# A gated linear-attention block with a ternary FFN on one core: probabilities, attention rows and first-norm rows split as rows and turned by transposing transfers

## The reference

```python
def step(carry, inp):
    mem, z = carry
    q_s, k_s, v_s = inp
    sq = jax.nn.elu(q_s) + 1.0
    att_mem = sq @ mem / (sq @ z)
    sk = jax.nn.elu(k_s) + 1.0
    mem = mem + jnp.einsum('bhlk,bhlv->bhkv', sk, v_s)
    z = z + sk.sum(axis=-2, keepdims=True).transpose(0, 1, 3, 2)
    att_dot = jax.nn.softmax(jnp.einsum('bhik,bhjk->bhij', q_s, k_s) * scale, axis=-1)
    att = att_dot @ v_s
    att = gate * att_mem + (1.0 - gate) * att
    return ((mem, z), att)
...
x = _layernorm(x + _L0_attn_ref(x, ...))     # its output: outs @ Wo
h = jax.nn.relu(jnp.einsum('bsd,fd->bsf', x, Wq1) + b1)
x = _layernorm(x + jnp.einsum('bsf,df->bsd', h, Wq2) + b2)
```

## Time and profile before

| | |
|---|---|
| median of 3 runs | 1882.06 us (1880.45 to 1883.52) |
| the profiled execution | 1882.23 us, its span 1880.3 us |
| TensorE busy | 1836.9 us, 98% |
| VectorE, ScalarE, GpSimd busy | 1448.7, 1004.3, 772.1 us (77%, 53%, 41%) |
| transfers | 117.47 MB in 556420 packets, 32.7% of 16 engines' time |
| mean granted clock of TensorE | 0.994 of full |

### The profile page before, as it was taken

One profiled execution on the slowest core, in us unless ns is written; L12 is line 12 of the kernel. 1 busy time (PEld: TensorE's weight loads), 2 busy tenths in 40 slices (PEclk: granted clock), 3 DMA queues, 4 the chain that ended last, 5 costly groups with the idle time before them and its releaser, 6 DMA issues.

```text
span 1880.3 us, 44342 instructions
## 1 busy us (share of the span) xinstructions
PE 1836.9 (98%) x16447; PEld 1305.1 (69%) x16447; DVE 1448.7 (77%) x2927; ACT 1004.3 (53%) x2422; POOL 772.1 (41%) x775
## 2 busy tenths in 40 slices
PE   5789999999999999999999999999999999999998
PEld 3666677776677776677776677776677776677765
DVE  7767877778877777877778877778877778877774
ACT  5765555555555555555555555555555555555541
POOL 1214334444334444334444334444334444334442
PEclk9899999999999999999999999999999999999999
DMA  8422433423433333333323343323333323333110
GB/s 274 125 39 37 65 59 62 67 42 56 67 59 60 67 47 51 66 57 62 68 42 56 66 60 60 67 41 57 65 62 60 67 39 59 61 63 63 34 24 23
DMA packets 556420, 117.47 MB, mean 62 GB/s; under 512 B 529824, under 2 KB 533808, under 8 KB 555696
## 3 DMA queue, kind: packets, MB, share of 16 engines
q1 hardware_dynamic: 556208, 114.64, 32.7%
HBM read 50.54 MB, written 16.80 MB: 36 GB/s over the span
## 4 chain that ended last, share of the span: by engine, by line
PE 95%; DVE 3%; ACT 1%; DMA 1%; POOL 0%; issue 0%; POOLq 0%; SPq 0%; DVEq 0%; ACTq 0%
PE bank L462 12%; PE bank L463 12%; PE bank L446 12%; PE bank L447 12%; PE bank L282 6%; PE bank L283 6%; PE bank L284 6%; PE bank L296 3%; PE bank L425 3%; PE bank L426 3%; PE bank L427 3%; PE bank L377 3%; PE bank L349 3%; PE bank L298 3%; PE bank L297 3%; PE bank L412 2%
## 5 line engine op out<-in xcount | busy, mean ns | idle before, releaser
L446 PE MATMUL bank<-yt,w1t 128*128 128x256 f16 x2048 | 453.9, 273 | 0.2 <-DVE yt L828 0.2
L447 PE MATMUL bank<-yt,w1t 128*128 128x256 f16 x2048 | 453.9, 273 | 0.0
L1157 ACT ACTIVATE prob<-bank,exp_bias,gscalars 128x128 f32<-128x128 f32 x512 | 227.7, 455 | 348.6 <-DVE exp_bias L745 346.8
L462 PE MATMUL bank<-w2t,arena 128*128 128x512 f16 x1024 | 388.4, 379 | 0.0
L463 PE MATMUL bank<-w2t,arena 128*128 128x512 f16 x1024 | 388.1, 379 | 0.0
L1201 ACT ACTIVATE arena<-bank,b_scaled,wscalars 128x256 f32<-128x256 f32 x512 | 262.9, 570 | 194.9 <-PE bank L447 123.8
L1326 POOL TENSOR_TENSOR att_mem<-att_mem,gate_in 128x512 f32<-128x512 f32 x60 | 76.2, 1271 | 356.7 <-DVE att_mem L784 356.7
L446 PEld LDWEIGHTS bank<-yt,w1t 128*128 128x128 f16 x2048 | 200.4, 98 | 23.4 <-ACT w2t L1226 0.3
L447 PEld LDWEIGHTS bank<-yt,w1t 128*128 128x128 f16 x2048 | 200.4, 98 | 22.8
L880 DVE CAST arena<-arena 128x512 f16<-128x512 f32 x256 | 159.6, 624 | 53.1 <-ACT arena L1201 52.4
L1404 POOL TENSOR_TENSOR arena<-arena 128x512 f16<-128x512 f32 x128 | 155.3, 1213 | 73.9 <-DVE arena L880 73.9
(11 more groups left out here) (184 smaller groups left out, 4324.5 us busy)
## 6 DMA issues: line engine op xcount, KB each, us to landing
rows<-in_L_attn_x SPq DMA_DIRECT2D x32, 512.0 KB, 3.9
out_rows<-rows SPq DMA_DIRECT2D x64, 256.0 KB, 2.3
x_blocks<-in_L_attn_x SPq DMA_DIRECT2D x248, 64.0 KB, 3.1
sk<-sk_t SPq DMA_DIRECT2D x480, 32.0 KB, 2.0
att_dot<-att_mem SPq DMA_DIRECT2D x480, 32.0 KB, 2.0
y_blocks<-rows SPq DMA_DIRECT2D x480, 32.0 KB
arena<-in_L_ffn_W SPq DMA_DIRECT2D x6, 1024.0 KB, 5.9
w2t<-in_L_ffn_W SPq DMA_DIRECT2D x2, 1024.0 KB, 13.1
```

The lines of the kernel that those rows point to most:

```text
L446: pe.matmul(ps[:, c], w1t[:, k, cols], yt[:, g % 2, :, k], start=k == 0, stop=False)
L447: ins = pe.matmul(ps[:, c], w1t[:, k, cols], yt[:, g % 2, :, KT + k], start=False, stop=k == KT - 1)
L462: pe.matmul(banks[own][:], h_hi[:, f, toks], w2t[:, f, :], start=f == 0, stop=False)
L1157: ins = act.activation(prob[:, t, at], ps[:, c], ACT.Exp, scale=gcol(g, G_EXP), bias=exp_bias[:, t, at:at + 1], accum_out=row_sum[:, t, h: ...
```

## The change

Three things are turned by a transposing transfer (`dma_start_transpose`) from SP, and their split into hi and lo is made before the turn, in rows:

- Probabilities: the exponentials write into the bank of the scores itself. `p_hi` (ScalarE) copies the bank to p_rows in float16, `p_lo` (VectorE) writes the rest beside it, and one transfer per sequence turns 128x2048 values into pt. TensorE's `turn_p` is gone, and a bank of scores is free only after p_lo.
- Attention rows and first-norm rows of groups 1 to 30: `at_hi`, `at_lo`, `yt_hi`, `yt_lo` work on rows, and one transfer per sequence turns 128x1024 values. The block moves and VectorE's turns of both are gone. The edge groups stay on TensorE.
- Order: both `scores` stand together on TensorE, then four pieces of `ffn_down`, then the V projections; VectorE has both score_max of a sequence together, group_max behind the first norm, and the p_lo between them; ScalarE has yt_hi in the middle of the exponentials and at_hi earlier; GpSimd has yt_lo before gate_mix.

```diff
@@ TensorE
             def scores(g, t):
-                    bank_free[b] = (sem["pexp"], by_half(g, t, e))
+                    bank_free[b] = (sem["pt_lo"], by_half(g, t, e))
-            def turn_p(g, t, half):
-                b = take(("p", g, t, half))
-                ps = banks[b][:].rearrange("p (h t) -> p h t", h=4)
-                pe.wait_ge(sem["pexp"], by_half(g, t, half))
-                for i in range(4):
-                    ins = pe.transpose(ps[:, i], prob[:, t, 4 * half + i], ident32[:])
-                ins.then_inc(sem["pturn"], 1)
-                bank_free[b] = (sem["pt"], by_half(g, t, half))
             def attend(g, t):
-                pe.wait_ge(sem["pt"], by_half(g, t, 1))
+                pe.wait_ge(sem[f"pt{t}"], 16 * (g + 1))
             def project_out(g, t):
-                pe.wait_ge(sem["at"], by_t(g, t))
+                pe.wait_ge(*at_there(g, t))
             def ffn_up(g, j):
-                pe.wait_ge(sem["yt"], by_t(g, 1))
+                pe.wait_ge(*yt_there(g, 0))
+                pe.wait_ge(*yt_there(g, 1))
@@ TensorE's loop
                 scores(g, 0)
+                scores(g, 1)
+                ffn_down(g - 2, 0, 0)
+                ffn_down(g - 2, 0, 1)
+                ffn_down(g - 2, 0, 2)
+                ffn_down(g - 2, 0, 3)
                 project_v(g, 0)
-                ffn_down(g - 2, 0, 0)
-                project_v(g, 1)
-                turn_p(g, 0, 0)
-                ffn_down(g - 2, 0, 1)
-                ffn_down(g - 2, 0, 2)
-                scores(g, 1)
+                project_v(g, 1)
                 read_memory(g, 0)
                 read_memory(g, 1)
-                ffn_down(g - 2, 0, 3)
                 ffn_down(g - 2, 1, 0)
                 ffn_down(g - 2, 1, 1)
-                turn_p(g, 0, 1)
-                turn_p(g, 1, 0)
                 turn_y(g - 1, 0)
-                turn_p(g, 1, 1)
@@ VectorE
-            def p_split(g, t, half):
-                ps = banks[bank_of["p", g, t, half]][:].rearrange("p (h t) -> p h t", h=4)
+            def p_lo(g, t, half):
+                ps = banks[bank_of["score", g, t, half]][:].rearrange("p (h t) -> p h t", h=4)
                 dve.wait_ge(sem["pt_hi"], by_half(g, t, half))
+                dve.scalar_tensor_tensor(out=p_rows[:, t, 1, hs], in0=ps, scalar=2.0 ** 13, in1=p_rows[:, t, 0, hs], op0=ALU.mult,
+                                         op1=ALU.subtract).then_inc(sem["pt_lo"], 1)
@@ ScalarE
             def exponentials(g, t, half):
-                    act.wait_ge(sem["pturn"], by_half(g - 1, t, half))
-                    ins = act.activation(prob[:, t, at], ps[:, c], ACT.Exp, ...
+                    ins = act.activation(ps[:, c], ps[:, c], ACT.Exp, ...
+            def p_hi(g, t, half):
+                if g:
+                    act.wait_ge(sem[f"pt{t}"], 16 * g)
+                act.wait_ge(sem["pexp"], by_half(g, t, half))
+                act.activation(p_rows[:, t, 0, 4 * half:4 * half + 4], ps, ACT.Copy, scale=2.0 ** 13).then_inc(sem["pt_hi"], 1)
@@ ScalarE's loop
                 exponentials(g, 0, 0)
+                p_hi(g, 0, 0)
+                exponentials(g, 0, 1)
+                p_hi(g, 0, 1)
+                if g - 1 not in EDGES:
+                    yt_hi(g - 1, 0)
+                    yt_hi(g - 1, 1)
+                exponentials(g, 1, 0)
+                p_hi(g, 1, 0)
+                exponentials(g, 1, 1)
+                p_hi(g, 1, 1)
                 v_split(g, 0)
@@ SP
+            def turn_p(g, t):
+                sp.wait_ge(sem["pt_lo"], by_half(g, t, 1))
+                if g:
+                    sp.wait_ge(sem["pv"], by_t(g - 1, t))
+                sp.dma_start_transpose(pt[:, t].rearrange("p c h n -> p (c h) n"),
+                                       p_rows[:, t].rearrange("p c h n -> p (c h n)")).then_inc(sem[f"pt{t}"], 16)
+            def turn_y(g, t):
+                sp.wait_ge(sem["yt_lo"], by_middle(g, t))
+                sp.dma_start_transpose(yt[:, g % 2, t], y_rows[:, t].rearrange("p c n -> p (c n)")).then_inc(sem[f"yt{t}"], 16)
+            def turn_att(g, t):
+                sp.wait_ge(sem["at_lo"], by_middle(g, t))
+                sp.wait_ge(sem["wo"], by_t(g - 1, t))
+                sp.dma_start_transpose(at[:, t], att_split[:, t].rearrange("p c n -> p (c n)")).then_inc(sem[f"at{t}"], 16)
@@ SP's loop
                 bounce_out(g + 1)
-                move_y(g - 1)
+                turn_p(g, 0)
+                turn_y(g - 1, 0)
+                turn_y(g - 1, 1)
+                turn_p(g, 1)
                 bounce_back(g + 1)
                 move_sk(g)
-                move_att(g)
+                turn_att(g, 0)
+                turn_att(g, 1)
                 put_out(g - 2, 0)
```

More of the change, by code:

```diff
@@ L32 @@
     amax amax_row amax_cell amax_all xscale sc0 sc1 sc2 sc3
-    xblocks ablocks yblocks skblocks xturn xt_hi xt kproj qproj kq_exp klo qlo elu vproj v_hi v1 v
-    score rowmax exp_bias pexp pturn pt_hi pt skturn
+    xblocks skblocks xturn xt_hi xt kproj qproj kq_exp klo qlo elu vproj v_hi v1 v
+    score rowmax exp_bias pexp pt_hi pt_lo pt0 pt1 skturn
     reset_fill reset mem num den attm invsum mix pv attd gated_in gated mixed upd
-    aturn at_hi at wo b2_scaled res0 bn0 mv0 var0 rstd0 norm0 yturn yt_hi yt yb
+    aturn at_hi at_lo at at0 at1 wo b2_scaled res0 bn0 mv0 var0 rstd0 norm0 yturn yt_hi yt_lo yt yt0 yt1 yb
     ffn1 relu h_hi h_dve h_pool ffn2 res1 bn1 mv1 var1 rstd1 norm1
@@ L863, in normalise @@
                                   ALU.mult).then_inc(sem[f"norm{which}"], 1)
-            def turn_y(g, t):
-                if not 0 < g < NG - 1:
-                    return
-                dve.wait_ge(sem["yblocks"], moved(g))
-                dve.transpose(y_blocks[:, t], y_blocks[:, t]).then_inc(sem["yturn"], 1)
             def h_split(g, j):
@@ L1019, in _ @@
                 score_max(g, 0, 0)
-                group_max(g + 1)
+                score_max(g, 0, 1)
                 normalise(g - 1, 0, 0)
+                normalise(g - 1, 1, 0)
                 if g == 0:
                     gates()
-                normalise(g - 1, 1, 0)
-                score_max(g, 0, 1)
+                group_max(g + 1)
+                p_lo(g, 0, 0)
+                score_max(g, 1, 0)
+                p_lo(g, 0, 1)
+                score_max(g, 1, 1)
                 if g >= LIVE:
@@ L1028, in _ @@
                     mem_add(g - 1, 1)
+                p_lo(g, 1, 0)
                 turn_x(g + 1, 0)
@@ L1033, in _ @@
                     ffn_scale()
+                p_lo(g, 1, 1)
+                v_split(g, 0)
                 turn_sk(g)
-                v_split(g, 0)
                 if g == 0:
@@ L1180, in yt_hi @@
                     return
-                if g >= 2:
-                    act.wait_ge(sem["ffn1"], 8 * (g - 2) + 8)
-                act.wait_ge(sem["yturn"], by_t(g, t))
-                act.activation(yt[:, g % 2, t, 0:KT], turned_y(g, t), ACT.Copy).then_inc(sem["yt_hi"], 1)
+                if g in EDGES:
+                    if g:
+                        act.wait_ge(sem["ffn1"], 8 * (g - 2) + 8)
+                    act.wait_ge(sem["yturn"], by_edge(g, t))
+                    ins = act.activation(yt[:, g % 2, t, 0:KT], turned_y(g, t), ACT.Copy)
+                else:
+                    if g > 1:
+                        act.wait_ge(sem[f"yt{t}"], 16 * (g - 1))
+                    act.wait_ge(sem["norm0"], by_t(g, t))
+                    ins = act.activation(y_rows[:, t, 0], rows[:, g % NX, t], ACT.Copy)
+                ins.then_inc(sem["yt_hi"], 1)
             def h_relu(g, j):
@@ L1241, in _ @@
                 h_relu(g - 2, 4)
+                if g - 1 not in EDGES:
+                    at_hi(g - 1, 0)
+                    at_hi(g - 1, 1)
                 qk_split(g, "k", 0)
@@ L1244, in _ @@
                 h_relu(g - 2, 5)
-                at_hi(g - 1, 0)
+                if g - 1 in EDGES:
+                    at_hi(g - 1, 0)
                 if g == 0:
@@ L1250, in _ @@
                     gates()
-                at_hi(g - 1, 1)
+                if g - 1 in EDGES:
+                    at_hi(g - 1, 1)
                 h_relu(g - 2, 6)
@@ L1275, in _ @@
                         put_w(n)
-                exponentials(g, 1, 0)
-                exponentials(g, 1, 1)
-                p_split(g, 0, 1)
+                v_split(g, 1)
                 if g == 0:
+                    w_sum(2, 0)
                     w_sum(2, 1)
@@ L1282, in _ @@
                         put_w(n)
-                p_split(g, 1, 0)
-                yt_hi(g - 1, 0)
+                if g - 1 in EDGES:
+                    yt_hi(g - 1, 0)
                 if g == 0:
-                    for n in range(4, 8):
+                    for n in range(4, 12):
                         put_w(n)
-                p_split(g, 1, 1)
-                if g == 0:
-                    for n in range(8, 12):
-                        put_w(n)
```

(3 more changed lines are left out.)

122 lines of the change are left out of this document (49 added, 73 removed).

## The result

| | before | after |
|---|---|---|
| median | 1882.36 us, 4 runs | 1892.95 us, 4 runs (1889.57 to 1893.36) |
| ratio | | 1.0053, 95% interval 1.0036 to 1.0071 |
| the profiled execution | 1882.23 us | 1893.2 us, its span 1891.4 us |
| TensorE busy | 1836.9 us, 98% | 1801.1 us, 95% |
| mean granted clock | 0.994 | 0.982 |

The change is slower by 10.6 us; the forecast was 31 us faster. TensorE is busy for 35.8 us less and the run is longer: it now waits.

The account below looks back on a forecast made before the run. TensorE, busy for 98% of the span and never resting in the steady loop, was taken as the bound. 1882.2 - 56.0 (turns gone) + 25 (bank wait) = 1851 us, range 1824 to 2070.

Parts of the forecast that it names:

- the bank wait: TensorE stands before read_memory until the last p_lo frees its bank: 0.8 us a group, 25 us over 31 groups.
- So 2.35 a half: ScalarE's time for one half's exponentials and p_hi, 1.87 plus 0.48 us; 9.4 for four halves.
- some 5 us either way: In group 0 attends now wait for transfers; some 5 us either way, inside the range.
- The change on TensorE: 512 turn_p instructions leave TensorE's queue: 1.75 us a group, 56.0 us over 32 groups.
- The transfers: Six transposing transfers a group on SP replace 32 block moves; attend loses nothing up to 4.4 us per large transfer.
- P: Time of one 512 KB transposing transfer on SP's queue, taken as under 4.1 us.
- SP late: Rival: P above 4.4 us, so attend(g,1) on TensorE waits for the second probabilities; 1886 to about 2100 us, chance 0.28.
- the serial turn: Rival: transfers turn small blocks one after another at block-move price, P = 12.7 us, 2667 us in all; chance 0.14.
- That one is free: The first V projection on TensorE wants its bank at 949.2, after the first p_lo ends near 947: no wait.
- Banks take the gain: Rival, no change: TensorE waits 1.6 to 1.9 us a group for banks, 1876 to 1886 us; chance 0.06.

Follow-up runs that it names:

- the load alone: Changed kernel with, in group 0, the load of a part of W2 issued on SP ahead of both second-sequence transfers: 1889.92 us, ratio 1.0039.
- five extra matmuls: Changed kernel plus five matmuls with discarded sums beginning the second V projection in groups 2 to 31: 1878.23 us; with two instead of five, 1879.89 us.
- the fastest kernel: Changed kernel with one piece of ffn_down ahead of read_memory and group 0's load of a part of W2 issued earlier: 1837.44 us, ratio 0.9761.
- the three orders tried: Changed kernel, early W2 load: old order in groups 0 and 1, 1897.61 us; ffn_down piece ahead, old order in group 1, 1840.72; also its put_w earlier, 1843.19.

## Why the prediction was wrong, point by point

The sum had one loss against the 56 us, the bank wait at 25, and three steps of it failed. The bank wait came to 38 us instead of 25 ("So 2.35 a half"). The clock, at nothing in the sum, took 11.8. The first two groups, put at "some 5 us either way" and at nothing in the sum, took 17.1. That is 42 us more than forecast, and the 31 us of gain became 11 us of loss in the profiled execution. That 1893 lies inside the range of 1824 to 2070 is luck: the range reached that far for a late SP, which did not come.

- **The change on TensorE: right.** 1.75 us a group were forecast; with no wait in the loop it is 54.70 against 56.41, 1.71 less.
- **The transfers: right.** Forecast: P under 4.1 us, limit 4.4, no wait for pt. The queue and the landing times of the changed kernel:

```profile
905.01 1.79 SPq L1542 DMA_TRANSPOSE pt<-p_rows  x1
906.90 3.38 SPq L1551 DMA_TRANSPOSE yt<-y_rows  x2
910.95 3.60 SPq L1542 DMA_TRANSPOSE pt<-p_rows  x1
914.64 0.53 SPq L1515 DMA_DIRECT2D amax_row<-amax_dram  x1
```
```profile
pt<-p_rows SPq DMA_TRANSPOSE x64, 5.5
at<-att_dot SPq DMA_TRANSPOSE x60, 3.1
```

  All four take 9.5 us of the queue, so P is 3.2. SP late and the serial turn, 0.42 of the chances, were wrong: what sixteen block moves cost says nothing of one turning transfer. By the Trainium skill's 261 GB/s (DMA: Bandwidth & Descriptors, Latency and other measured facts) a transfer of 512 KB takes an estimated 2.0 us. The queue's 1.79 and 3.60 lie on both sides of it, but the landing comes 5.5 us after the issue, which the bandwidth alone does not give. The Trainium skill has 1309 ns for one 128x128 turn by transfer (VectorE: DVE Perf Modes, The three transpose paths), by which sixteen one after the other would take an estimated 21 us. The trace does not bear that out for one transfer of sixteen: it landed after 5.5.
- **The bank wait: the mechanism right, the term too small.** "So 2.35 a half" failed. Four exponentials and the p_hi take 2.45 (955.16 to 957.61), because p_hi starts 0.10 after the last read has ended at 957.02, a gap that the sum left out:

```profile
955.16 0.43 ACT L1137 ACTIVATE bank<-bank,exp_bias,gscalars 128x128 f32<-128x128 f32 x1 [7.34 <-DVE exp_bias L742]
...
956.82 0.20 ACT L1137 ACTIVATION_READ_ACCUMULATOR bank<-bank,exp_bias,gscalars 128x1 f32 x1
957.12 0.60 ACT L1148 ACTIVATE p_rows<-bank 128x512 f16<-128x512 f32 x1
957.61 0.43 ACT L1137 ACTIVATE bank<-bank,exp_bias,gscalars 128x128 f32<-128x128 f32 x1
...
960.06 1.14 ACT L1175 ACTIVATE y_rows<-rows 128x512 f16<-128x512 f32 x2
```

  That is 0.4 us over four halves; the wait is 1.13, not 0.8. An exponential that writes a bank is not the reason: it takes 0.43 us, against 0.46 in the earlier trace rows. The 29 loops of 55.90 are 36 us over what 54.66 each would give, and in the last read_memory waits 1.8 us; the term was 25.
- **The clock: a term that was missing.** The text had it only as something on top of a late SP. A wait of 1.13 us was enough: 11.8 us. The earlier trace rows showed a low clock only in the first slices, and I took a short wait for just its length.
- **"That one is free": failed in groups 0 and 1.** I reckoned the V projection on a group of the middle, with four pieces of ffn_down ahead of it. In groups 0 and 1 there is no group g-2, and V comes straight behind the scores: 6.51 and 4.58 us.
- **"In group 0 ... some 5 us either way": failed.** I looked for attends that wait for transfers. None does; what waits is the load behind the transfers on SP, and the sums on ScalarE and VectorE that stand behind the probabilities. The start lost 13.6 us and won nothing of its own 3.5, 17.1 in all: 12.0 are more idle time of TensorE, and the rest goes with the lower clock, 0.87 against 0.93. By the medians the load accounts for 3 to 5 us; for some 10 the cause stays open, see the last section.
- **The chances.** "Banks take the gain", the right place, had 0.06 and reached 1886. It needed 0.33 us more a group, and a clock and a start that were in no rival.

The sum that holds: 1882.2 - 56.0 + 36 + 1.8 + 11.8 + 17.1 = 1892.9, against 1893.2 in the profiled execution.

## What to carry to other kernels

An engine that is 98% busy in a loop has a price for idle time that is more than the idle time: here 36 us of waits cost another 12 of clock, and 0.43 us of useless matmuls a group won all of it back. A sum made on one group of a steady loop has to be made again for the groups where a neighbour in the order is missing, and on each queue for what stands behind the moved work. A transposing transfer in place of TensorE's turns pays once something else is put where the new wait would be (40 us here, 44.6 with the load moved too).

## What the runs showed of the hardware that was not expected

The granted clock fell in kernels whose loops wait 1.13 us (7 times in the changed kernel, 9 with the load alone), and not in those with 0.69 or 0.56 us, one trace of each (the latter has two single waits of 0.92 and 0.94 us, without a fall). In the changed kernel the falls are 225.3 us apart. Why only about one group in four falls, although all have the same wait, these runs don't show.

The first two groups of one and the same code differ from trace to trace: the changed kernel has its second project_out at 158.1, the runs that differ from it only in later groups at 154.5 (five extra matmuls) and 156.9 (two). With the load moved, the first project_out is at 99.0 to 102.8 in four traces whose code is the same up to there. TensorE stands much there, and the clock is low for parts of it, so a start is known to some 4 us from one trace; of the 17.1 above as much is unsure. Some 10 us of it are left in the fastest kernel (151.3 against 141.0, which is 144.5 less twice 1.75), and what would win them stays open: the three orders tried only moved the wait.
